# Cross attention with transposed scores: the product computed twice, no transposes of probabilities

## The reference

```
q = (Q @ Wq + bq), k = (K @ Wk + bk), v = (V @ Wv + bv)     # 16 heads of 8
scores = einsum('bhqd,bhkd->bhqk', q, k) / sqrt(8)
scores = where(mask == 0, -inf, scores)                      # mask (1, 1, 256, 512)
attn = softmax(scores, axis=-1)
ctx = einsum('bhqk,bhkd->bhqd', attn, v);  out = ctx @ Wo + bo
```

## Time and profile before

| | us |
|---|---|
| median of 3 runs | 208.26 (208.04 to 213.51) |
| the profiled execution | 207.73 |
| its span | 205.9 |
| PE busy | 195.0 (95%) |
| DVE busy | 152.7 (74%) |
| ACT busy | 132.2 (64%) |
| POOL busy | 100.3 (49%) |
| PE in the chain that ended last | 68% |

### The profile page before, as it was taken

How to read it: one execution, slowest core, us unless ns; L and a number is a source line. 1 busy time by engine, 2 the same in 40 slices (tenths; PEclk the granted TensorE clock), 3 DMA queues, 4 the chain that set the end, 5 groups by cost and what they waited for, 6 DMA issues and landing times.

```text
span 205.9 us, 4419 instructions
## 1 busy us (share of the span) xinstructions
PE 195.0 (95%) x1562; PEld 152.1 (74%) x1562; DVE 152.7 (74%) x405; ACT 132.2 (64%) x308; POOL 100.3 (49%) x149
## 2 busy tenths in 40 slices
PE   7999999999999899996999999999989999999993
PEld 7678876678777667864666757575668799999993
DVE  2576787577559788579999999999973866448752
ACT  2475458697679649279998898987976232553220
POOL 7589207757673887905769991003300017420422
PEclk9999999999999999999999999999999999999999
DMA  6980477989636002533004100000000000001000
GB/s 149 392 212 4 153 102 98 129 113 125 83 58 207 14 5 66 86 99 135 0 18 113 25 3 0 2 5 0 0 3 0 3 2 3 0 0 29 0 0 25
DMA packets 10948, 12.67 MB, mean 62 GB/s; under 512 B 952, under 2 KB 8888, under 8 KB 10856
## 3 DMA queue, kind: packets, MB, share of 16 engines
q1 hardware_dynamic: 10112, 11.28, 25.9%
q10 hardware_dynamic: 720, 0.93, 1.3%
q0 software_dynamic: 96, 0.20, 0.7%
HBM read 10.96 MB, written 1.44 MB: 60 GB/s over the span
## 4 chain that ended last, share of the span: by engine, by line
PE 68%; DVE 10%; ACT 9%; issue 4%; POOL 4%; DMA 3%; ACTq 0%; POOLq 0%; DVEq 0%
PE ps L926 13%; PE ps L887 8%; PE ps L947 7%; PE ps L813 7%; PE ps L829 6%; PE ps L702 6%; PE ps L785 5%; PE ps L864 5%; PE ps L846 4%; ACT q_t L624 3%; PE ps L715 3%; DMA biases<-in_biases 3%; ACT prob L590 2%; PE ps L904 2%; DVE q_t L1149 2%
## 5 line engine op out<-in xcount | busy, mean ns | idle before, releaser
L479 POOL TENSOR_TENSOR prob<-prob,rec 128x512 f32<-128x512 f32 x32 | 32.4, 1040 | 23.5 <-DVE rec L1202 23.5
L1149 DVE CUSTOM_DVE_ANT_0 q_t<-ps,mask_add 128x512 f32<-128x512 f32 x64 | 41.3, 683 | 3.3 <-PE ps L846 2.0
L590 ACT ACTIVATE prob<-ps,low 128x256 f32<-128x256 f32 x64 | 29.7, 489 | 10.5 <-DVE low L1139 10.5
L624 ACT ACTIVATE q_t<-q_t,low 128x512 f32<-128x512 f32 x44 | 29.3, 716 | 4.2 <-DVE low L1149 4.1
L515 POOL TENSOR_TENSOR place_k<-place_k 128x256 f32<-128x256 f32 x14 | 10.2, 731 | 39.1 <-DVE place_k L1173 39.1
L1139 DVE TENSOR_REDUCE low<-ps 128x2 f32<-128x512 f32 x32 | 20.4, 683 | 8.5 <-PE ps L785 8.5
L887 PEld LDWEIGHTS ps<-ident,q_t 128*128 128x128 f32 x176 | 19.6, 141 | 8.7 <-ACT q_t L624 2.9
L887 PE MATMUL ps<-ident,q_t 128*128 128x128 f32 x176 | 23.7, 276 | 2.1 <-ACT place_k L660 0.8
L610 ACT ACTIVATE q_t<-ps 128x512 f32<-128x512 f32 x18 | 10.6, 599 | 21.0 <-PE ps L926 21.0
L1189 DVE TENSOR_TENSOR q_t<-q_t,ps 128x512 f32<-128x512 f32 x18 | 12.2, 684 | 11.5 <-PE ps L926 8.6
L829 PE MATMUL ps<-ident,prob 128*128 128x128 f32 x128 | 18.4, 278 | 1.5 <-POOL prob L479 0.9
(11 more groups left out here) (173 smaller groups left out, 429.7 us busy)
## 6 DMA issues: line engine op xcount, KB each, us to landing
k_stack<-k_dram SPq DMA_DIRECT2D x9, 256.0 KB
wg<-in_L_ffn_w_gate SPq DMA_DIRECT2D x1, 1024.0 KB, 22.0
wu<-in_L_ffn_w_up SPq DMA_DIRECT2D x1, 1024.0 KB, 31.8
q_stack<-q_dram SPq DMA_DIRECT2D x6, 144.0 KB
k_dram<-prob SPq DMA_DIRECT2D x1, 768.0 KB, 3.6
w_in<-in_L_attn_Wq ACTq DMA_DIRECT2D x2, 256.0 KB, 5.8
context<-in_ctx SPq DMA_DIRECT2D x1, 512.0 KB, 6.0
w_in<-in_L_attn_Wv SPq DMA_DIRECT2D x1, 512.0 KB, 7.6
```

The costliest lines, as they stand in the source:

```text
L479: nc.gpsimd.tensor_tensor(pr, pr, rec1[:, s % 2, r, :].unsqueeze(2).to_broadcast([P, C, S]), ALU.mult).then_inc(s_norm1, 1)
L590: e = nc.scalar.activation(prob1[:, s % 3, r, c * S:(c + 1) * S], ps[:, 2 * (s % 2) + r, c * S:(c + 1) * S], ACT.Exp, bias=low1[:, s % 2, ...
L624: nc.scalar.activation(prob2[n % 3][:, c, :], score2[n % 2][:, c, :], ACT.Exp, bias=low2[:, n % 2, c:c + 1], scale=-1.0).then_inc(s_exp2, 1)
L1149: nc.vector.tensor_tensor_reduce(out=score2[n % 2][:, c, :], in0=ps[:, 2 * (n % 2) + c, :], in1=mask_add[:, c, :], scale=1.0, scalar=3e38, ...
```

## The change

- Scores are computed twice. The first product is as before (queries on partitions, keys along the row) and serves only to find the maximum. The second has keys on partitions: 128 keys x 256 queries, so that its exponential, read from PSUM, is already what the value products need. Transposes and copies of probabilities are gone, and so are the sums' places; prob2 disappears.
- The maximum enters the second product as two extra rows: the negated maximum as a bf16 part and a rest, against two rows of ones in the key stack. DVE writes both as columns of a small tile (shift_cols), PE turns them with an identity product, ACT copies two rows into q2_stack, one copy for each head of a pair.
- The mask enters as a product of an identity with the transposed mask in bf16, which starts the accumulation of each bank.
- Six combinations of parts instead of nine: 48 rows and the two extra ones. A pair of heads lies in two tiles of 64 rows (partitions 0 and 64). The loop runs over 16 pairs, j = g - CROSS_G, with the first product LEAD = 3 pairs ahead. Its results use three banks (S_BANK), the second product and the shifts three others (E_BANK) in rotation.
- The key stack is filled from SBUF to SBUF by 12 transfers to 8 partitions each, without DRAM; the exponential that waited for d_kdram waits for all of them. The queries' parts go to DRAM in six transfers instead of one, and come back in four instead of six.
- The expert weights are laid out on the host as they are needed and come in three loads. GpSimd splits the first 8 of 18 weights in steps 8 to 15 of the self attention, behind its divisions, and the rest from step CROSS_G + 2 on.
- The transposed mask is one more load, and DVE makes its additive form between the evacuations of the last two key blocks. GpSimd fills the ones, zeros, bf16 identity and shift columns ahead of its wait for the value weights.

The diff, cut to its core:

```diff
-KSTACK = PARTS * PARTS * HD2
+H2P = H2 // 2
+Q_RUNS = ((0, 3), (0, 1), (0, 2))
+K_ROWS = (0, 0, 0, 2, 1, 1)
+ROW_TILE, SHIFT_ROWS = 64, 2
+STACK = SHIFT_ROWS + len(K_ROWS) * HD2
...
+CROSS_G = N_SELF + 2
+LEAD = 3
+LAST_G = CROSS_G + N_PAIRS + 1
...
+def exp_units():
+    order = [("shift", 0)]
+    for j in range(N_PAIRS):
+        order += [(2 * j + r, 0) for r in range(2)]
+        if j + 1 < N_PAIRS:
+            order.append(("shift", j + 1))
+        order += [(2 * j + r, 1) for r in range(2)]
+    return {x: v for v, x in enumerate(order) if x[0] != "shift"}, {
+        x[1]: v for v, x in enumerate(order) if x[0] == "shift"}
+S_BANK, E_BANK, RING = 0, 3, 3
+VALUES2 = {CROSS_G + 2 * k + 2: k for k in range(N_GROUPS)}
+O_READY = {g + 1: k for g, k in VALUES2.items()}
+SPLIT_G, SPLITS_EARLY, SPLIT_LATE_G = 8, 8, CROSS_G + 2
+FFN_G, FFN_EARLY = CROSS_G + N_PAIRS - 1, 3
...
-QSETS = ((0, 4), (4, H2))
+QSETS = ((0, 2), (2, H2P))
 # SP
-            load(k2_dram.rearrange("j r t -> r j t"), k2_parts, d_kdram)
-            sp.wait_ge(d_kdram, 16)
-            for j in range(PARTS):
-                for i in range(PARTS):
-                    r = (j * PARTS + i) * HD2
-                    load(k2_stack[r:r + HD2, :, :], k2_dram[j].rearrange("(d h) t -> d h t", d=HD2), d_kstack)
+            for i in range(2):
+                for p, part in enumerate(K_ROWS):
+                    row = ROW_TILE * i + SHIFT_ROWS + p * HD2
+                    load(k2_stack[row:row + HD2, :, :], k2_parts[ROW_TILE * i:ROW_TILE * (i + 1), part, :], d_kstack)
...
+                for first, last in Q_RUNS:
+                    for i in range(2):
+                        load(q2_dram[b, i, p:p + last - first].rearrange("p r t -> r p t"),
+                             q2_parts[ROW_TILE * i:ROW_TILE * (i + 1), first:last, :], d_qdram[b])
+                    p += last - first
+                sp.wait_ge(d_qdram[b], 16 * 2 * len(Q_RUNS))
 # ACT
-                    if s == 1 and r == 1:
-                        act.wait_ge(d_kdram, 16)
+                    if s == 0 and r == 0:
+                        act.wait_ge(d_rows, 16 * 4)
+                    elif s == 1 and r == 1:
+                        act.wait_ge(d_kstack, 16 * 2 * len(K_ROWS))
...
+            def shift_rows(j):
+                act.wait_ge(s_shiftps, j + 1)
+                b, s = divmod(j, H2P)
+                for i in range(2):
+                    rows = slice(ROW_TILE * i, ROW_TILE * i + SHIFT_ROWS)
+                    ins = nc.scalar.copy(q2_stack[rows, s, b * S:(b + 1) * S],
+                                         ps[rows, E_BANK + SHIFT_UNIT[j] % RING, 0:S])
+                ins.then_inc(s_exp2, 1)
+            def exp2(n, half):
+                v = EXP_UNIT[n, half]
+                act.wait_ge(s_score2t, 4 * (n // 2) + 2 * half + n % 2 + 1)
+                if n >= PT_SLOTS:
+                    act.wait_ge(s_pv2, n // HG - 1)
+                nc.scalar.activation(prob2_t[n % PT_SLOTS][:, 2 * half:2 * half + 2, :],
+                                     ps[:, E_BANK + v % RING, :].rearrange("p (k t) -> p k t", k=2), ACT.Exp
+                                     ).then_inc(s_exp2, 1)
 # ACT's loop: output copy if g in O_READY (waits for the value products), then
+                if 0 <= j < N_PAIRS:
+                    for r in range(2):
+                        exp2(2 * j + r, 0)
+                    if j + 1 < N_PAIRS:
+                        shift_rows(j + 1)
...
+                if 0 <= j < N_PAIRS:
+                    for r in range(2):
+                        exp2(2 * j + r, 1)
 # PE
+            def scores2(j, c):
+                b, s = divmod(j, H2P)
...
+                for r in range(2):
+                    u = 4 * j + 2 * c + r
+                    if u >= RING:
+                        pe.wait_ge(s_top2, u - RING + 1)
+                    else:
+                        pe.wait_ge(s_exp1, 2 * (N_SELF - 2) + u + 1)
+                    t = b * S + c * P
+                    mm(ps[:, S_BANK + u % RING, :], q2_stack[rows_of(r), s, t:t + P],
+                       k2_stack[rows_of(r), s, b * SK:(b + 1) * SK], start=True, stop=True).then_inc(s_score2, 1)
+            def exp_bank_free(v):
+                if v >= RING:
+                    pe.wait_ge(s_exp2, v - RING + 1)
...
+            def shift_rows(j):
+                v = SHIFT_UNIT[j]
+                exp_bank_free(v)
...
+                pe.wait_ge(s_shift2, j + 1)
+                for c in range(C):
+                    last = mm(ps[:, E_BANK + v % RING, c * P:(c + 1) * P], shift_cols[:, j % 2, c, :], ident_b[:, :],
+                              start=True, stop=True)
+                last.then_inc(s_shiftps, 1)
+            def mask_scores(j, half):
...
+                for r in range(2):
+                    v = EXP_UNIT[2 * j + r, half]
+                    exp_bank_free(v)
+                    mm(ps[:, E_BANK + v % RING, :], ident_b[:, :],
+                       mask_t_add[:, 2 * half:2 * half + 2, :].rearrange("p k t -> p (k t)"), start=True, stop=False)
+            def scores2_t(j, half):
+                b, s = divmod(j, H2P)
+                if half == 0:
+                    pe.wait_ge(s_exp2, SHIFT_UNIT[j] + 1)
+                for r in range(2):
+                    v = EXP_UNIT[2 * j + r, half]
+                    for k2 in range(2):
+                        t = b * SK + (2 * half + k2) * P
+                        last = mm(ps[:, E_BANK + v % RING, k2 * S:(k2 + 1) * S], k2_stack[rows_of(r), s, t:t + P],
+                                  q2_stack[rows_of(r), s, b * S:(b + 1) * S], start=False, stop=k2 == 1)
+                    last.then_inc(s_score2t, 1)
 # PE's loop, in the order of the queue
+                if 0 <= j < N_PAIRS:
+                    mask_scores(j, 0)
+                if g in O_READY:
+                    turn_outputs2(O_READY[g])
+                if 0 <= j < N_PAIRS - 1:
+                    shift_rows(j + 1)
...  # self attention steps and BETWEEN
+                if 0 <= j < N_PAIRS:
+                    scores2_t(j, 0)
+                if 0 <= j + LEAD < N_PAIRS:
+                    scores2(j + LEAD, 0)
+                    scores2(j + LEAD, 1)
+                if j == -1:
+                    shift_rows(0)
+                    for b, p in WO1.get(g, ()):
+                        out_proj1(b, p)
+                if 0 <= j < N_PAIRS:
+                    mask_scores(j, 1)
+                    scores2_t(j, 1)
                 if FFN_G <= g < FFN_G + FFN_EARLY:
                     expert_step(g - FFN_G)
+                if g in VALUES2:
+                    for kc in range(KC):
+                        values2(VALUES2[g], kc)
 # DVE
+                elif (kind, which) == ("k", 6):
+                    dve.wait_ge(d_mask_t, 16)
+                    nc.vector.tensor_scalar(mask_t_add[:, :, :], mask_t, 0, MASKED, ALU.is_equal, ALU.mult
+                                            ).then_inc(s_maskadd, 1)
...
+            def top_scores2(j):
+                for u in range(4 * j, 4 * j + 4):
+                    c, r = divmod(u % 4, 2)
+                    dve.wait_ge(s_score2, u + 1)
+                    if u >= 2:
+                        dve.wait_ge(s_top2, u - 1)
+                    nc.vector.tensor_tensor_reduce(out=score2[u % 2], in0=ps[:, S_BANK + u % RING, :],
+                                                   in1=mask_add[:, c, :], scale=1.0, scalar=-3e38,
+                                                   op0=ALU.add, op1=ALU.max, accum_out=top2[:, j % 2, c, r:r + 1]
+                                                   ).then_inc(s_top2, 1)
...
+                link(nc.vector.tensor_scalar(cols[:, :, :, 0], top2[:, j % 2, :, :], -1.0, None, ALU.mult))
+                nc.vector.scalar_tensor_tensor(out=cols[:, :, :, 1], in0=top2[:, j % 2, :, :], scalar=-1.0,
+                                               in1=cols[:, :, :, 0], op0=ALU.mult, op1=ALU.subtract
+                                               ).then_inc(s_shift2, 1)
...
 # POOL
+                if SPLIT_G <= g < SPLIT_G + SPLITS_EARLY:
+                    split_weights(g - SPLIT_G)
```

316 lines of the change are left out of this document (142 added, 174 removed).

## The result

The changed kernel takes **243.7 us** (median of 4 executions, 242.7 to 248.3), against 208 us before: 1.169 times, 95% interval 1.164 to 1.175. The forecast was 221.5 (206 to 237): the direction was right, the size was not, and the time lies above the range. The profiled execution took 243.1 us, 241.3 of it the span.

What follows compares the result with a forecast made beforehand. Cross attention was taken as bound by DVE, ACT and PE near their limit, then by waits in PE's in-order queue. 207.7 + 0.25 (mask) + 8.4 (entry) + 4.6 (loop) + 0.6 (third expert) = 221.5 us, range 206 to 237.

Steps and rivals of the forecast that it cites:

- the doubtful zero: Self attention: the twelve key stack pieces land by 30 us, so the exponential at 32.34 waits for nothing, cost zero.
- rival 1: Self attention: key stack late at 74 GB/s, landing at 44.3, exponential waits 12 us; 233.5 us (228 to 241), chance 0.25.
- The loop: Cross attention: waits in TensorE's in-order queue make four heads take 9.05 us against 8.1, +4.6 us in all.
- a: Cross loop, every pair: first half to second half, with the fourth score product waiting for its maximum, 2.15 us.
- b: Cross loop, end of a pair: next shift product waits for the last exponential's bank, 1.65 us.
- c: Cross loop, every second pair: value products, output copy and turn, shift and transposed products stand between, 3.1 us.
- The entry: Cross attention start: first exponential at 98.0 us, from 84.4 + 7.2 + 4.3 + 2.1, costing +8.4 us.
- Rivals 2 and 3: Loop at TensorE's busy sum, 6.9 us; 2: shorter entry, 201.4 us, chance 0.13; 3: forecast's entry, 207.4 us, chance 0.10.
- the sign: Whole kernel: slower, chance 0.77, against faster 0.13 and same 0.10.
- the second mask: Self attention: converting the transposed mask on DVE delays a key evacuation and the fourth value product group, +0.25 us.
- weights and weight splits: Fused weight loads and GpSimd's eight early splits in the self attention cost nothing; splits up to 1 us if cover fails.
- the third expert's 0.6: Experts: the third expert stands behind the last value block as today, +0.6 us.

Runs made afterwards that it cites:

- experiment 2: Changed kernel with the key parts first written to DRAM and the twelve transfers reading from there, the exponential waiting only for the write: 230.7 us, 1.107.
- experiment 3: Changed kernel with the twelve key stack transfers reordered so pieces for the lower and upper 64 partitions take turns: 242.8 us, 1.168.
- experiment 6: On experiment 1's version, the last two of a pair's four score products moved behind the second half's transposed products: 223.2 us, 1.075.
- experiment 5: Changed kernel with the next pair's shift product moved behind a pair's first transposed products: 244.9 us, 1.175.
- experiment 13: On experiment 1's version, 6.9 us of products added: half the mask products twice (by ratio level with experiment 1), or every score product twice (3.9 us above the mask run).
- experiment 1: Changed kernel with the key parts in their own SBUF place, so no exponential waits for the key stack: 228.4 us, 1.098.
- experiment 8: Changed kernel with key parts in their own place, shift product, last two score products and output copy and turn all later: 220.7 us, 1.059.
- experiment 4: Changed kernel with the two loads of the experts' weights held back until the key stack has landed: 240.0 us, 1.146.
- experiments 10: Score products issued three times where TensorE waits for maxima: on experiment 1's version 226.7 us, 1.088; on experiment 8's version 224.8 us, 1.077.
- 12: Experiment 1's version without mask products, each transposed product issued twice and some score products three times: 244.7 us, 1.166.

## Why the prediction was wrong

**The step that failed** is the key stack: "landed by 30: nothing. This is the doubtful zero". It was costed with the rate of a write from 128 partitions (3.6 us for half the bytes), though the same rows held a price for pieces of eight partitions, 74 GB/s, and the rival built on it named the place and the wait, 12 us. That the wait agrees to the tenth is in part luck: alone the pieces run at 86 GB/s and land by 40.0, and the weights beside them, which the rival did not count, make up the rest to 44.1. The argument that spoke for the optimistic row, that the slow part may be the read, was wrong (experiment 2). The port rule quoted for the rival stays open: spreading the pieces over both halves did not help (experiment 3), but each still reached only its two or three ports. Of two rows for one unknown, the one with the same shape at the end that is written was the nearer. With rival 1 as the forecast, the same sum gives 233.5.

**What came with it:** 3.15 us of half clock after the stall. The prediction named a clock below 1.0 as an uncounted cost, for the cross stage; here the stall of every engine brought it in the self attention.

**The loop: mechanism right, size off.** The three segments were there with the waits named: 9.53 us against 9.05 (a 2.25 for 2.15, b 1.79 for 1.65, c 3.23 for 3.1). Where the tenths lie, the timeline of TensorE in this turn shows:

```profile
158.88 0.44 PE L969 MATMUL ps<-ident,o_raw 128*128 128x128 f32 x2
159.15 0.28 PE L921 MATMUL ps<-ident_b,shift_cols 128*128 128x128 bf16 x2
159.36 0.40 PE L944 MATMUL ps<-q_stack,k_stack 50*128 50x256 bf16 x4
159.59 0.59 PE L900 MATMUL ps<-k_stack,q_stack 50*128 50x512 bf16 x3
160.75 0.39 PE L900 MATMUL ps<-k_stack,q_stack 50*128 50x512 bf16 x1 [0.58 <-DVE top L1245]
161.07 0.60 PE L932 MATMUL ps<-mask_t_add,ident_b 128*128 128x512 bf16 x2
161.61 0.40 PE L944 MATMUL ps<-q_stack,k_stack 50*128 50x256 bf16 x4
```

In a the wait for the maximum (1.16 us from the first score product to the fourth, forecast 1.18) and the two masks (0.54 for 0.51) were right; the fourth score product stands alone, shares the array with none, and takes 0.32 us with its change of shape to the masks, not the 0.12 of one in a pair. The shift product takes 0.21 with its change (159.15 to 159.36), forecast 0.11, in b and c. A change of shape is then about 0.1 us (0.32 less 0.215), where 0.08 was taken. The Trainium skill (TensorEngine Tiling (Array Packing), Key Properties) has a change of mode drain the engine; the 0.1 agrees with there being a price. Eight turns at 9.53 are 3.8 us more than forecast; the other 2.3 of the 6.1 are left over for the clock, 0.93 over the loop; that they are its is argued, not measured apart. That the fourth score product's wait is real was shown by experiment 6, that b and c share their slack with a by experiment 5: the segments were right as a description of one order, but not as independent prices.

**The entry: right but 1.85 short.** Its three terms can be read one by one:

```profile
105.67 0.60 PE L900 MATMUL ps<-k_stack,q_stack 50*128 50x512 bf16 x3
...
110.06 0.28 PE L921 MATMUL ps<-ident_b,shift_cols 128*128 128x128 bf16 x2
```

Pair 1's scores come 7.37 us after pair 0's (forecast 7.2), the shift 4.39 later (4.3), and the first exponential 3.69 after that (2.1). So the maxima were sized right, and 1.6 of the 1.85 lie in the last term, where the clock is 0.54 and projection, masks and transposed products run slow (1.93 instead of 1.06 for the first of them). In experiment 13's mask run the clock is full there, and the entry takes 14.37 us with a mask product more, against 15.7 in experiment 1: the half clock is 1.3 us of it.

**Rivals 2 and 3** (a pace of TensorE's busy sum, 6.9) did not come. Even with the queue's waits gone, four heads take 8.2 to 8.65 us (experiment 8).

**Right:** the sign; the second mask, weights and weight splits worth nothing, which experiment 1 shows together (first cross product at 83.42 against 83.39); in the changed kernel, where the exponential waits for the pieces, the weights beside them do cost some 4 us (experiment 4); the third expert's 0.6.

What stays open: what exactly lowers the clock (added products went with a higher one in experiments 10 and 13, but not in 12), what halves an engine's rate into eight partitions, and whether pieces of 16 would land in time.

## What to carry to other kernels

When a wait is moved onto a transfer, price the transfer by the row whose written side has the same shape, and give a zero that hangs on a better row no more weight than its rival. Taking one wait out of an in-order queue only moves the time if another wait in the same turn is fed by what is now later: take out the one whose work nothing else in the turn depends on, and then try the first again. Before taking work away from TensorE, look at how near it is to losing its clock: here 13.8 us of products taken out cost 6. And when equal work is added in two places, compare the turns at full clock before calling a difference one of the clock.

## What the runs showed that was not expected

- Leaving out 64 full-height bf16 products (13.8 us) made the kernel 6 us slower: mean clock 0.89 instead of 0.967. Adding 32 such products (6.9 us) left the time unchanged: nearly half of their time fell into waits, and the clock of 0.985 to 0.998 paid for the rest.
- The clock falls without a long stop: in the changed kernel TensorE's longest wait in 98 to 110 us is 0.78 us, and from 110 to 113 the clock is 0.55.
- One program varied from 223.0 to 233.0 us with its clock (0.992 and 0.934), so gains of 2 us can't be told apart in this kernel by a few executions.
- Each of twelve SBUF-to-SBUF transfers took SP 0.6 us to issue (7.84 in all), the same pieces from DRAM 0.3 (4.02).
